# Attention with a mixture of experts on one core: the product with the values in two halves around the turned scores

## What is computed

```python
q = _qdq(x) @ _qdq(wq).T + bq
kv = cond @ wkv.T + bkv
k, v = jnp.split(kv, 2, axis=-1)
attn = jax.nn.softmax(jnp.einsum('bnhd,bmhd->bhnm', q, k) * scale, axis=-1)
o = jnp.einsum('bhnm,bmhd->bnhd', attn, v).reshape(B, N, C)
out = _qdq(o) @ _qdq(wp).T + bp
```

## Time and profile before

| | us |
|---|---|
| median of 3 runs | 407.78 |
| lowest and highest | 407.14, 410.28 |
| span of the profiled execution | 405.0 |
| PE busy in it | 358.6 (89%) |
| DVE busy | 303.5 (75%) |
| ACT busy | 250.9 (62%) |
| POOL busy | 124.1 (31%) |

### The profile page before, as it was taken

The page is one execution under the profiler, slowest core; times in us unless marked ns, Lnnn a source line. Parts: engine busy times, 40 slices in busy tenths (PEclk is TensorE's granted clock), DMA queues, the critical chain, the costliest instruction groups (busy, mean ns, idle before and its releaser), DMA issues.

```text
span 405.0 us, 14019 instructions
## 1 busy us (share of the span) xinstructions
PE 358.6 (89%) x5793; PEld 269.3 (67%) x5793; DVE 303.5 (75%) x656; ACT 250.9 (62%) x412; POOL 124.1 (31%) x116
## 2 busy tenths in 40 slices
PE   0896899999998998998999999998864699999993
PEld 0663468668677766855866776786643587888882
DVE  3888886775776676586577668668896877999993
ACT  3476477777686676776768666567721535666761
POOL 6151462132022122222203300001101054787870
PEclk9999699999999999999999999999985858999998
DMA  7869965565294186166336208544000009635001
GB/s 253 196 157 197 241 146 134 87 159 136 58 171 115 53 152 182 54 106 175 103 61 125 54 14 142 129 137 141 3 2 2 1 1 306 191 116 163 2 0 45
DMA packets 34512, 45.65 MB, mean 113 GB/s; under 512 B 3995, under 2 KB 30299, under 8 KB 34323
## 3 DMA queue, kind: packets, MB, share of 16 engines
q1 hardware_dynamic: 33395, 43.74, 44.5%
q0 software_dynamic: 640, 0.78, 0.9%
q10 hardware_dynamic: 416, 0.26, 0.3%
HBM read 25.08 MB, written 0.47 MB: 63 GB/s over the span
## 4 chain that ended last, share of the span: by engine, by line
PE 76%; DVE 13%; issue 5%; ACT 2%; POOL 2%; DMA 1%; DVEq 0%; ACTq 0%; POOLq 0%
PE PS L1035 35%; PE PS L1101 9%; PE PS L1078 8%; PE PS L1112 7%; PE PS L1363 4%; PE PS L1322 3%; DVE mx L794 2%; PE PS L1088 2%; PE PS L1346 2%; PE PS L1312 1%; DMA x_in<-x 1%; DVE KN L743 1%; PE PS L1279 1%; DVE st L697 1%; DVE mtop L798 1%
## 5 line engine op out<-in xcount | busy, mean ns | idle before, releaser
L794 DVE TENSOR_REDUCE mx<-PS 112x1 f32<-112x500 f32 (+1 forms) x128 | 114.3, 933 | 52.8 <-PE PS L1078 52.7
L501 ACT ACTIVATE PT_all<-PS 128x1344 f32<-128x1344 f32 x64 | 82.6, 1290 | 10.1 <-PE PS L1101 9.9
L1035 PE MATMUL PS<-cT,wkvT 128*128 128x500 f16 x288 | 71.5, 385 | 18.0 <-POOL slot_of L404 11.2
L1035 PE MATMUL PS<-wkvT,cT 128*125 128x256 f16 x576 | 73.2, 279 | 0.0
L1035 PEld LDWEIGHTS PS<-wkvT,cT 128*125 128x125 f16 x576 | 65.3, 139 | 5.3 <-issue 0.5
L395 POOL TENSOR_TENSOR cT<-c_in,cT 128x1000 f16<-128x1000 f32 x18 | 37.5, 2082 | 86.9 <-ACT cT L479 86.9
L1035 PEld LDWEIGHTS PS<-cT,wkvT 128*128 128x128 f16 x288 | 27.5, 99 | 50.8 <-POOL slot_of L404 11.2
L486 ACT ACTIVATE KN<-PS,col_in 128x500 f16<-128x500 f32 x48 | 32.5, 677 | 40.6 <-PE PS L1035 40.6
L1078 PE MATMUL PS<-arena,QC 96*112 96x500 f16 x192 | 52.4, 380 | 3.1 <-issue 2.8
L1101 PE MATMUL PS<-QC,arena 98*128 98x112 f16 x768 | 49.2, 214 | 3.0 <-ACT QC L521 2.9
L493 ACT ACTIVATE V<-PS 125x512 f32<-125x512 f32 x48 | 28.7, 598 | 30.6 <-PE PS L1035 30.6
(11 more groups left out here) (207 smaller groups left out, 463.8 us busy)
## 6 DMA issues: line engine op xcount, KB each, us to landing
arena<-KN SPq DMA_DIRECT2D x144, 125.0 KB, 3.6
c_in<-ctx SPq DMA_DIRECT2D x24, 500.0 KB, 4.5
cT<-W SPq DMA_DIRECT2D x11, 352.0 KB
c_in<-W SPq DMA_DIRECT2D x6, 352.0 KB
cT<-W SPq DMA_DIRECT2D x11, 176.0 KB
arena<-place_far SPq DMA_DIRECT2D x1, 1568.0 KB, 10.0
c_in<-W SPq DMA_DIRECT2D x6, 176.0 KB
PT_all<-L_xattn_wkv SPq DMA_DIRECT2D x1, 512.0 KB, 6.1
```

The source lines that it names most:

```text
L501: act.activation(PT_all[:, u % 4, :].rearrange("p (c k) -> p c k", c=CH), PS[:, 3:6, 0:4 * TP], ACT.Exp, scale=SCORE).then_inc(s["exp_done ...
L794: dve.tensor_reduce(mx[:, u % 2, k:k + 1], PS[0:TP, k:1 + k * (CH - 1), 0:CW], AX.XY, ALU.max).then_inc(s["red_done"], 1)
L1035: ins = mm(out_, w(a, h), x_(b, h), start=first and k == 0, stop=last and k == len(todo) - 1)
```

## The change

The product with the values of the odd slots 3 to 55 is no longer one block of 48 matmuls ahead of the turned scores. Its first six key tiles (24 matmuls) stand where it stood, the other six behind the turned scores of the same slot and ahead of the next slot's scores. The evacuation of its bank on ACT moves from the end of the slot to the next slot, behind that slot's first step, the exponential, and ahead of its first evacuation. `outputs` falls away; `half_outputs`, which was there for the last slots, is used instead.

```diff
--- before.py
+++ after.py
@@ -509,10 +509,8 @@
                 kind, n, u = use
                 if kind == "K":
                     keys_hi(n, u)
-                elif kind == "V":
+                else:
                     evacuate_values(n, u)
-                else:
-                    outputs_evac(u)
 
             def augment(u):
                 b, i = divmod(u, NPAIR)
@@ -537,13 +535,16 @@
                 fills = slot_fills(u)
                 if 2 <= u:
                     exp(u - 2)
+                before = slot_fills(u - 1) if u > 0 else []
+                if len(before) > 1 and before[1][0] == "P":
+                    outputs_evac(before[1][2])
                 if fills and fills[0]:
                     evacuate(fills[0])
                 if 1 <= u <= SLOTS:
                     augment(u - 1)
                 if i % 2 == 1 and i < 6 and b + 2 < B:
                     context_hi(b + 2, i // 2)
-                if len(fills) > 1:
+                if len(fills) > 1 and fills[1][0] != "P":
                     evacuate(fills[1])
                 if u < SLOTS:
                     for g, half in late_halves(u):
@@ -1102,18 +1103,6 @@
                               QC[0:QR + 2, b % 2, i * TP:(i + 1) * TP], start=True, stop=True)
                 last.then_inc(s["t_ready"], 1)
 
-            def outputs(g):
-                b, hg = divmod(g, 4)
-                need(pe, "exp_done", 2 * g + 2)
-                need(pe, "v_done", 6 * (b + 1))
-                bank = take(("P", 0, g))
-                for t in range(KT):
-                    for j in range(4):
-                        last = mm(PS[32 * j:32 * j + VW, bank, 0:S], V[:, b % 2, t, 4 * hg + j, :],
-                                  PT[:, (2 * g + j // 2) % 4, t * TP + (j % 2) * S:t * TP + (j % 2 + 1) * S],
-                                  start=t == 0, stop=t == KT - 1, tile_position=(0, 32 * j))
-                last.then_inc(s["pv_ready"], 1)
-
             def half_outputs(g, half):
                 b, hg = divmod(g, 4)
                 need(pe, "exp_done", 2 * g + 2)
@@ -1131,10 +1120,8 @@
                 kind, n, u = use
                 if kind == "K":
                     project_keys(n, u)
-                elif kind == "V":
+                else:
                     project_values(n, u)
-                else:
-                    outputs(u)
 
             def turn_weights():
 
@@ -1174,13 +1161,18 @@
                     project(fills[0])
                 if 1 <= u and not early:
                     turn_maxima(u - 1)
-                if len(fills) > 1:
+                split = len(fills) > 1 and fills[1][0] == "P"
+                if split:
+                    half_outputs(fills[1][2], 0)
+                elif len(fills) > 1:
                     project(fills[1])
                 if u < SLOTS:
                     for g, half in late_halves(u):
                         half_outputs(g, half)
                 if 1 <= u <= SLOTS:
                     turned_scores(u - 1)
+                if split:
+                    half_outputs(fills[1][2], 1)
                 if u >= SLOTS:
                     for g, half in late_halves(u):
                         half_outputs(g, half)
```

## The result

| | before | changed |
|---|---|---|
| median of 6 runs, us | 410.12 | 418.60 |
| lowest and highest | 407.14, 410.99 | 418.37, 421.15 |
| span of the profiled execution | 405.0 | 418.2 |

The ratio is 1.0238, with a 95% interval of 1.0196 to 1.0279. The changed kernel measured once more gave 1.0225 (1.0157 to 1.0293). The three runs of before shown ahead of the prediction had a median of 407.78; with 13 to 19 runs it is 409.5 to 410.1, since nearly all runs of this kernel scatter from 406 to 415 us. The two profiled executions lie 13.2 us apart, the medians 8.5. What follows is read from the traces, and the medians are taken up again at the end.

A forecast was written before the change was run, and what follows sets the result against it. The prediction took PE to bound the kernel: 14 V slots at 0.53 us plus 12 K slots at 0.61 add 14.7 us to the 407.78 median, giving 422.5 us, range 413 to 426.

The forecast's parts named there:

- PE bounds the slots: From 57 to 272 us PE works 209.11 of 215.00 us, so anything making it late in a slot costs in full.
- The rival that another engine sets the pace: DVE's reductions, maxima and key steps bound the slots, so PE's delay fills idle time: +0, 407.8 us; chance 0.06.
- The wait: Before an odd slot's turned scores, PE idles until QC is filled: 0.32 us in V slots, 0.40 in K slots.
- The rival in which QC is in time: In odd slots QC is ready early enough and only matmul mode switches cost: 0.21 us each, 413.3 us; chance 0.08.
- The turns: Full-width/column-tiled switches around the second half: 0.14 us between starts entering it, 0.14 taken for leaving to the scores.
- the upper bound: From second half to next scores, at most 0.18 us: the scores' whole 0.13 weight load on top of 0.05.
- The rival in which the turns are hidden: In odd slots mode switches cost nothing but PE still waits for QC: 9.3 us, 417.1 us; chance 0.10.
- The evacuation behind the exponential: ACT's output copy (L506, 0.22 us), moved behind the next slot's exponential, is covered and costs 0.
- Sum 14.7: Over odd slots 5 to 55: 14 V slots at 0.53 us plus 12 K slots at 0.61 make +14.7 us.
- The halts stay as they are: The forecast took nothing off for PE's halts of 1 to 2 us in the slots, within 5.89 us idle.
- halts gone: PE's slot halts may come of 96 records issued at one go; splitting saves at most 5.9 us: 416.6; chance 0.06.
- The clock stays: A lower clock is not likely to add time: at the end of the slots PE runs at 1.00 despite waits.

The follow-up runs named there:

- two ways of taking it away: Changed kernel with QC filled before the projection's evacuation in odd slots, ratio 1.0085; changed kernel with the product cut after 10 of 12 key tiles, 1.0006.
- 128 waits: Kernel before with 128 more semaphore waits at the head of PE's stream, where PE waits for its first data anyway: median 403.97 us, ratio 0.9844.
- small transfers: Kernel before with key stacking (from batch 2) and context loads (from batch 3) moving 100 of each 500 columns: median 404.55 us, ratio 0.9880.
- back-to-back halves: Kernel before with its product written as two halves directly following each other, in the old order with the old evacuation: median 417.38 us, ratio 1.0173.
- 64 waits: Kernel before with 64 extra semaphore waits at the head of PE's stream: median 425.38 us, ratio 1.0380.

## Why the prediction was right, and where not

- **PE bounds the slots, and what delays it is paid in full.** Right: 26 waits, DVE and ACT wait longer for PE, nothing absorbs it. The rival that another engine sets the pace is out.
- **The wait, 0.32 and 0.40 us a slot, 9.3 us.** Right: 8.9 by two ways of taking it away. The rival in which QC is in time (413.3) is out. The view shows it as 0.24 and 0.32, since it counts from the modelled end of the last matmul; from start to start it is 143.61 + 0.72 = 144.33 to 144.65, 0.32.
- **The turns.** Mis-sized slightly: 5.5 us forecast, 6.8 measured. The exit to the scores costs 0.18 and not 0.14, which is 1.0 of the 1.3; the rest is roundings of 0.01 us a slot. The size of the upper bound was the true value. The rival in which the turns are hidden (417.1) is out, though by the median alone it would have looked better than the forecast.
- **The evacuation behind the exponential, 0.** Right (208.2 with it alone).
- **Sum 14.7.** The slots cost 15.7: 0.4 less for the wait, 1.3 more for the turns, 0.1 of rounding.
- **The halts stay as they are.** Wrong, and this is the step that puts the median of 418.6 below the 422.5 forecast and the difference of the medians, 8.5 us, below the 14.7. The prediction had it as a rival with 0.06 (halts gone, 416.6), and the median of 418.6 lies nearer to that than to 422.5. But it explained them by the 96 records at one go, and those stand unsplit in the two kernels that lost their halts (128 waits, small transfers). The halts are stops of PE's instruction supply at borders of 256; the changed kernel keeps them small, 2 us against 7 to 12. The count of instructions does not do it (the back-to-back halves have the same count and 16.3 us), and at record 4546 more time between borders does not either (4.8 us against 4.9). Its packets of instructions begin 2 to 4 us sooner behind the border at 4546, 5826 and 7106; at the first two the traces show less busy queues. The wait on QC has a part in that (2.0 and 1.9 us with it, 3.8 and 7.8 without). That the new order would put borders and transfers apart could not be read from the rows of before; that it did so is luck as far as the forecast goes.
- **The clock stays.** Nearly: the slots ran at 0.99 to 1.00, but in both traces of the changed kernel PE ran at a low clock once near slot 57, which cost 1.1 and 1.2 us. The variants with the same halves do not show it, and no long stop goes ahead of it; its cause stays open.
- The medians: 407.78 was a low draw for before. The 8.5 us would be 15.7 less some 7 of halts, and the two pairs of traces give back 5.1 and 10.3. The other runs have no trace, so that the halts also make the ratio's interval 0.8% wide is likely and not shown.

The version that beats both is the kernel before with the 128 waits, 403.97 us. It is bought by an alignment that any edit of PE's stream can undo.

## What to carry to other kernels

A block that seems to stand in another engine's way may be the cover of a wait: before splitting it, lay its length beside the copy that the next step needs. Where an engine is saturated and its halts repeat once per round with no releaser, count its instructions between them; if it comes out at a multiple of 256, compare variants with the halts taken out, and try a shift of the stream before judging a change of 1 to 2%.

## What the runs showed of the hardware

- PE's halts without a releaser stood in front of record 194 modulo 256 in every trace, from 0.5 to 4 us long, and PE went on 1.3 to 1.8 us behind the landing of a 16 KB packet on the instruction queue. The Trainium skill (Runtime: NRT & Kernel Launch, Instruction fetch mechanics) says that an engine's instructions are refilled in blocks of 256 by a DMA queue of its own, and that crossing a border is mostly hidden. The blocks agree with the counts. "Mostly hidden" holds by number, since 26 of the 32 borders of the kernel before cost less than 0.5 us, but not in sum: beside 8 MB of transfers the borders cost nothing, the same borders beside 25 MB 7 to 12 us, and badly placed ones 23.
- Halts of PE of up to 1.8 us left the granted clock at 1.00, 2.4 GHz (behind one of 1.6 us the projection took 1.44 us). Of the nine longer ones, 1.9 to 4 us, eight were followed by half speed, 1.2 GHz, for some 3 us or, twice, 7; one of 2.8 us, at 167 us with the 64 waits, was not. In the second trace of before this added 1.6 us to each of two halts of 2.
- A turn from full-width to column-tiled matmuls cost 0.09 us (0.14 from start to start instead of 0.05), the turn back to the scores 0.17 in sum (0.13 and 0.04 of the first long matmul).
